# Load lag, batch-statistics chain and first-strip order in the output stage of a two-layer convolution and gating kernel

## What is computed

```
n  = groupnorm(x)
xc = n * channel_gate                      # one factor per image and channel
g  = sigmoid(y) + sigmoid(s)               # one factor per image and pixel (a scan y, a 7x7 convolution s)
x2 = xc * g
mean, var = x2.mean((0, 1, 2)), x2.var((0, 1, 2))       # over all images: one pair per channel
out = x + relu((x2 - mean) * rsqrt(var + 1e-5) * gamma + beta)
```

## Time and profile before

| what | value |
|---|---|
| median of 3 runs | 3327.27 us |
| lowest and highest | 3323.25 and 3329.84 us |
| span of the profiled execution, first to last instruction | 3373.7 us |
| busy share of the span: PE, DVE, ACT | 77%, 88%, 80% |
| moved by the DMA engines | 1227.97 MB, mean 364 GB/s |

### The profile page before, as it was taken

The page is one execution under the profiler, slowest core; times in us unless marked ns, Lnnn a source line. Parts: engine busy times, 40 slices in busy tenths (PEclk is TensorE's granted clock), DMA queues, the critical chain, the costliest instruction groups (busy, mean ns, idle before and its releaser), DMA issues. The chain is left out here.

```text
span 3373.7 us, 50742 instructions
## 1 busy us (share of the span) xinstructions
PE 2587.4 (77%) x17105; PEld 1657.5 (49%) x17105; DVE 2976.3 (88%) x4060; ACT 2701.0 (80%) x3772; POOL 56.8 (2%) x111
## 2 busy tenths in 40 slices
PE   7899999999999999999976333333776776766676
PEld 5566666666566666665432000000555555555555
DVE  8788999889998889988886999998999899888787
ACT  6788888888888888887763888887888888877777
POOL 3000000000000000000001100000000000000000
PEclk9999999999999999999986555555877778777767
DMA  8899999999999999998755999996999999999997
GB/s 318 328 374 399 386 367 366 364 368 401 374 364 365 369 398 384 366 367 335 274 129 122 380 420 419 420 421 261 382 428 430 428 426 420 415 386 374 373 369 289
DMA packets 199056, 1227.97 MB, mean 364 GB/s; under 512 B 29792, under 2 KB 38936, under 8 KB 157644
## 3 DMA queue, kind: packets, MB, share of 16 engines
q1 hardware_dynamic: 195884, 1223.41, 91.1%
q0 software_dynamic: 2976, 2.00, 0.3%
HBM read 805.14 MB, written 420.17 MB: 363 GB/s over the span
## 5 line engine op out<-in xcount | busy, mean ns | idle before, releaser
L1440 PE MATMUL psum<-signs,taps 128*128 128x448 f16 x4032 | 855.4, 355 | 29.4 <-DVE signs L1071 14.4
L1554 PE MATMUL psum<-signs,picked 12*128 12x448 bf16 x896 | 334.4, 517 | 340.4 <-DMA signs<-gate_scratch 276.6
L1945 ACT ACTIVATE stage<-psum 128x512 f32<-128x512 f32 x784 | 407.5, 614 | 209.1 <-DMA out_dram<-stage 186.7
L1440 PEld LDWEIGHTS psum<-signs,taps 128*128 128x128 f16 x4032 | 386.8, 98 | 351.7 <-issue 33.8
L1965 DVE SCALAR_TENSOR_TENSOR xc<-xt,curs,psum 128x1792 f32<-128x1792 f32 x222 | 452.0, 2077 | 121.7 <-PE psum L1554 119.2
L835 ACT ACTIVATE xt<-psum 128x896 f32<-128x896 f32 x416 | 378.0, 910 | 151.8 <-PE psum L1338 128.0
L1757 DVE SCALAR_TENSOR_TENSOR xc<-xt,curs,psum 128x1792 f32<-128x1792 f32 x224 | 455.8, 2077 | 34.0 <-PE psum L1554 33.1
L1691 ACT ACTIVATE xc<-xc 128x1792 f32<-128x1792 f32 x224 | 380.0, 1697 | 95.9 <-DVE xc L1757 95.9
L1122 DVE CUSTOM_DVE_ANT_0 xt<-scratch,xt 128x896 f32<-128x896 int8 x416 | 435.7, 1084 | 14.2 <-ACT scratch L843 14.2
L1338 PE MATMUL psum<-ident,stage 128*128 128x128 f32 x3066 | 410.2, 276 | 16.4 <-DMA stage<-x_dram 10.6
L1933 ACT ACTIVATE xc<-xc,bn,curs 128x1792 f32<-128x1792 f32 x224 | 411.1, 1899 | 7.6 <-DVE xc L1965 4.2
(11 more groups left out here) (222 smaller groups left out, 2830.4 us busy)
## 6 DMA issues: line engine op xcount, KB each, us to landing
xt<-x_scratch SPq DMA_DIRECT2D x210, 1792.0 KB
out_dram<-stage SPq DMA_DIRECT2D x112, 1792.0 KB, 13.6
stage<-x_dram SPq DMA_DIRECT2D x219, 896.0 KB, 9.0
xc<-x_scratch SPq DMA_DIRECT2D x210, 896.0 KB, 8.2
x_scratch<-xt SPq DMA_DIRECT2D x208, 896.0 KB, 8.5
x_scratch<-last_unit SPq DMA_DIRECT2D x16, 896.0 KB, 8.9
signs<-ssm_scratch SPq DMA_DIRECT2D x14, 448.0 KB, 4.6
xc<-ssm_scratch SPq DMA_DIRECT2D x14, 448.0 KB, 5.0
```

Of the source, the lines that this page charges most:

```text
L1440: return nc.tensor.matmul(turn[h % 2][:, b * 512:b * 512 + HB], taps[:, j, t, :], signs[:, j, r:r + RT // 2, dw:dw + W], start=t == 0, sto ...
L1554: last = nc.tensor.matmul(dst[:, b, :], picked[:, b * P:(b + 1) * P], gate_rows[:, s * BW:(s + 1) * BW], start=True, stop=True)
L1945: nc.scalar.activation(outs[n % 2][:, 2 * k:2 * k + 2, :].rearrange("p t c -> p (t c)"), out_ps[k % 4], ACT.Identity).then_inc(staged, 1)
```

## The change

It has three parts, all around the end of the third stage and in the output stage.

1. **SP's stream of the output stage** is written out for all 112 strips instead of a loop. At strip m it waits for `x2_made`, loads the gate row of strip m + 7, and then loads the next strips of x as far as `behind` lets it: strips 7 to 27 are loaded 7 strips ahead as before, strips 28 to 48 six ahead, and strips 49 to 111 five ahead. The store follows as before. The gate rows have semaphores of their own, `gates4`, for which PE's `spread` waits; DVE's `make_u` now waits for `arrived4`, which counts strips of x alone.
2. **The statistics chain.** Products of the scales with 1 / (number of pixels) are made early in the third stage (`gains`, in the tile `pair_counts`), which turns three products and a later scaling into one product. The refinement of the reciprocal root has two instructions of another kind in place of three. The scale is put on all of `par` by one instruction in place of two. Only the first half of u of the first strip is made ahead of the reductions; the second comes behind the chain, and so does the copy of the first image's row of `par` into `curs`, which stood at the head of the next block.
3. **The first two strips.** At strips 0 and 1 PE spreads the gate of strip m + 2 behind the fourth group of transposes of strip m, and DVE makes u of strip m + 1 after it has added strip m (before: at strip 0 only).

```diff
@@ third stage, DVE
+                nc.vector.tensor_scalar(gains[:, :, 0:NJ], par[:, :, NJ:2 * NJ], 1.0 / (NB * HW), None, ALU.mult
+                                        ).then_inc(gains_made, 1)
...
+                nc.vector.tensor_tensor(gains[:, :, NJ:2 * NJ], gains[:, :, 0:NJ], par[:, :, NJ:2 * NJ], ALU.mult
+                                        ).then_inc(gains_made, 1)
...
-                for j in range(NJ):
+
+                def first_strip(j):
                     nc.vector.scalar_tensor_tensor(
...
+                first_strip(0)
...
-                steps(nc.vector.tensor_tensor(wsum[:, :, 0:NJ], bnsum[:, :, 0:NJ], scales, ALU.mult))
-                steps(nc.vector.tensor_tensor(wsum[:, :, NJ:2 * NJ], bnsum[:, :, NJ:2 * NJ], scales, ALU.mult))
-                steps(nc.vector.tensor_tensor(wsum[:, :, NJ:2 * NJ], wsum[:, :, NJ:2 * NJ], scales, ALU.mult))
+                dve.wait_ge(gains_made, 2)
+                steps(nc.vector.tensor_tensor(wsum[:, :, :], bnsum[:, :, :], gains, ALU.mult))
...
-                steps(nc.vector.tensor_scalar(bn[:, 0:2, :], bn[:, 0:2, :], count, None, ALU.mult))
...
-                steps(nc.vector.tensor_tensor(t, t, rs, ALU.mult))
-                steps(nc.vector.tensor_scalar(t, t, -0.5, 1.5, ALU.mult, ALU.add))
-                steps(nc.vector.tensor_tensor(rs, rs, t, ALU.mult))
+                steps(nc.vector.scalar_tensor_tensor(t, t, -0.5, rs, ALU.mult, ALU.mult))
+                steps(nc.vector.scalar_tensor_tensor(rs, t, 1.5, rs, ALU.add, ALU.mult))
...
+                nc.vector.tensor_copy(curs[:, 0:1, :], par[:, NB - 1:NB, :]).then_inc(cur_made4, 1)
+                first_strip(1)
@@ output stage, SP
+                def behind(m):
+
+                    return min((m - NS) * 5 // (total - NS), 2)
...
+                fetched = NS
+                for m in range(total):
+                    sp.wait_ge(x2_made, 2 * (m + 1) + X4)
+                    if m + NS < total:
+                        load_gate(sp, gates4, ((m + NS) // NS - 1) % NB, m % NS)
+                    while fetched < total and fetched - NS + behind(fetched) <= m:
+                        fetch(fetched)
+                        fetched += 1
+                    sp.wait_ge(staged, (m + 1) * TG + E4)
@@ output stage, PE
-                        if n + 2 < NN or more:
+                        early = isinstance(it, int) and it == 0 and n < 2
+                        if not early and (n + 2 < NN or more):
                             spread(it, n + 2)
...
+                            if early and k == 3:
+                                spread(it, n + 2)
@@ output stage, DVE
+                    dve.wait_ge(arrived4[s], it * 32 + 16 * (n // NS + 1))
...
-                        first = isinstance(it, int) and it == 0 and n == 0
-                        if not first and (n + 1 < NN or more):
+                        early = isinstance(it, int) and it == 0 and n < 2
+                        if not early and (n + 1 < NN or more):
```

More of the change, by code:

```diff
@@ L1838, in binary_conv_then_gated_ssm_block @@
         arrived4 = [sem(f"arrived4_{s}") for s in range(NS)]
+        gates4 = [sem(f"gates4_{s}") for s in range(NS)]
         spread4 = sem("spread4")
-        cur_made4 = sem("cur_made4")
         u_made4 = sem("u_made4")
@@ L1889, in spread @@
                 def spread(it, n):
-                    pe.wait_ge(arrived4[n % NS], it * 64 + 32 * (n // NS + 1))
+                    pe.wait_ge(gates4[n % NS], it * 32 + 16 * (n // NS + 1))
                     pe.wait_ge(u_made4, it * (2 * NN) + 2 * n)
@@ L1969, in _ @@
                 dve.sem_inc(x2_made, X4)
-                nc.vector.tensor_copy(curs[:, 0:1, :], par[:, bass.ds(place(0, 0), 1), :]).then_inc(cur_made4, 1)
                 dve.wait_ge(cur_made4, 1)
@@ L1985, in step @@
                                                     slots[n % NS][:, :, j, :], ALU.add).then_inc(x2_made, 1)
-                        if first:
+                        if early:
                             make_u(it, n + 1)
```

35 lines of the change are left out of this document (15 added, 20 removed).

## The result

The changed kernel took **3352.42 us** (median of 5 runs, 3336.21 to 3358.22); the kernel before took 3325.80 beside it (5 runs, 3317.86 to 3329.84). The ratio is 1.0077 [1.0062, 1.0092]: slower, where 3318.0 was forecast. The executions of both kernels fall in two groups and a ratio leaves out those more than 1.5% above the fastest of their kernel, so I give beside each ratio how many lay over 3340 us, and the median of all.

A forecast was written before the change was run, and what follows sets the result against it. Transfers were taken to bound the kernel, with DVE close behind. Head 2.9 us (chain 0.75, first strips 2.1) plus lag 6.2 made 9.1 us off the 3327.3 median: 3318.2, stated as 3318.0, range 3311 to 3326.

The forecast's parts named there:

- The statistics chain: End of third stage: shorter chain and one half of u made later start relu 0.75 us earlier, ends 0.75 and 1.75.
- The first two strips: Output stage's start: first store at R+15.8, not R+18.2 (R: ACT's first relu); 2.1 us gained, 3.3 with faster PE.
- the faster variant: First strips, if PE's clock has risen: additions of strip 2 end 0.6 us earlier than before, instead of 0.6 later.
- The head: Statistics chain and first two strips together: 2.9 us gained, ends 2.9 and 5.0, all carried to the end.
- The lag: Output stage: strips 21 and 43 without loads save 9.9 us, late loads cost 3.6; net 6.2, ends 5.1 and 7.4.
- the rival that the lag gives nothing back: Output stage: compute cannot use the strips without a load, so only the head's gain remains, 3324.4 us; chance 0.20.
- SP's written-out stream: Output stage: gate row ahead of the load issues the load about 1 us later, which costs nothing with the queue full.
- slower, by the rate of the transfers: Output stage: changed addresses start the slow pace at strip 43 instead of 66, costing 27 us less 9: 3345; chance 0.09.

The follow-up runs named there:

- e9: Changed kernel with SP's output-stage loop of before and no lag, keeping the new statistics chain and first strips; 3323.87 us, ratio 0.9995.
- second trace of before: The kernel before, unchanged, profiled a second time, in an execution without the slow stretch; its time 3330.64 us.
- e6: Kernel before, its loop kept, with only the gate row issued ahead of the load in the output stage; 3327.66 us, ratio 1.0012.
- e7: Kernel before with SP's output-stage loop written out as straight code and nothing else; 3342.09 us, ratio 1.0052.
- e3: Changed kernel without the lag: SP's stream written out, every strip loaded 7 strips ahead; 3358.38 us, ratio 1.0054.
- e2: Changed kernel, run again beside the kernel before on the same chip; 3345.13 us, ratio 1.0027.
- e10: Changed kernel with SP's loop of before and the lag inside it (strips 6 and 13 without a load, then five ahead); 3314.79 us, ratio 0.9950.
- e15: Repeat of e10 on another chip; 3318.27 us, ratio 0.9979.
- e14: Kernel before with SP's output-stage loop as 3 turns of 28 strips in place of 6 of 14; 3384.88 us, ratio 1.0169.

## Why the prediction was wrong, point by point

**The statistics chain: size wrong, on the good side.** The changed kernel, same view as the earlier trace rows:

```profile
2328.97 0.19 ACT L1695 ACTIVATION_READ_ACCUMULATOR xc<-xc  x1
2329.19 1.08 DVE L1787 TENSOR_REDUCE bnsum<-scratch 128x16 f32<-128x112 f32 x4
2330.30 0.22 DVE L1794 TENSOR_TENSOR wsum<-bnsum,pair_counts 128x64 f32<-128x64 f32 x1
...
2333.16 0.19 DVE L1810 TENSOR_TENSOR par<-par,bn 128x32 f32<-128x32 f32 x1
2333.39 0.17 DVE L1812 COPY curs<-par 128x4 f32<-128x4 f32 x1
2333.47 2.07 DVE L1778 SCALAR_TENSOR_TENSOR xc<-xt,curs,psum 128x1792 f32<-128x1792 f32 x1
2336.11 3.65 ACT L1951 ACTIVATE xc<-xc,bn,curs 128x1792 f32<-128x1792 f32 x2 [4.16 <-DVEq L1991]
```

From the last sum of squares (2329.16) to relu 6.95 us, before 2350.95 - 2342.38 = 8.57: 1.62 us gained. The prediction chose 0.75 between ends of 0.75 and 1.75. Relu began 0.57 us behind the end of u (2335.54), not 1.0 and a copy behind it, so most of the barrier ran beside u. With what the Trainium skill says of sequencer instructions (PSUM — Partial Sum Buffer, Engine vs sequencer instructions) this row agrees: the gain is near the 1.75 that followed from it.

**The first two strips: right, with one order missed.** Counted from R, now 2336.11:

```profile
2342.05 3.68 PE L1926 MATMUL psum<-ident,last_unit 128*128 128x128 f32 x16 [4.24 <-DVE last_unit L2002]
2345.93 4.02 DVE L2002 TENSOR_TENSOR signs<-xc,xt 128x1792 f32<-128x1792 f32 x2
...
2351.91 0.37 SPq L1897 DMA_DIRECT2D out_dram<-stage  x1
2352.76 0.67 SPq L1885 DMA_DIRECT2D xt<-x_scratch  x1
2354.09 0.93 PE L1554 MATMUL psum<-signs,picked 12*128 12x448 bf16 x4
2355.06 4.07 DVE L1984 SCALAR_TENSOR_TENSOR xc<-xt,curs,psum 128x1792 f32<-128x1792 f32 x2 [1.13 <-PE psum L1554]
```

The first store is at R+15.8, as forecast (before R+18.2). The load of strip 8 is at R+16.65 and not R+14.3, since SP was still waiting for strip 0's staging when it could have been issued; the program's order shows that, and I had not followed it for SP. The DMA share is 0.48 from 2350 to 2355 us and 1.00 or more from there to 2370, so the engines are full soon behind the first store, as forecast. The additions of strip 2 end at R+26.9, with PE at the quicker clock (spread 0.93 us where the earlier trace rows has 1.65), 0.8 earlier than before; the faster variant said 0.6. The head alone is e9: its executions under 3340 are 3.0 us under those of the kernel before beside it (3323.3 against 3326.3). The forecast was 2.9, but the nearness is partly luck: the ratio's interval, 0.9985 to 1.0006, takes in no change, and the chain gave more than its term while the first strips gave less. From R to the end the traces without a slow stretch and without lag take 977.1, 978.1 and 977.4 us with the old first strips (second trace of before, e6, e7), 974.8 and 977.4 with the new ones (e3, e9), 1.5 us less on average where 2.1 was forecast.

**The lag: right in mechanism, and in size as far as the spread lets one see.** DVE behind the load that strip 21 leaves out (strips 24 and 25), and the chain of waits around it:

```profile
2542.54 3.95 DVE L2002 TENSOR_TENSOR last_unit<-xc,xt 128x1792 f32<-128x1792 f32 x2
2546.52 4.07 DVE L1984 SCALAR_TENSOR_TENSOR xc<-xt,curs,psum 128x1792 f32<-128x1792 f32 x2
2550.51 3.95 DVE L2002 TENSOR_TENSOR signs<-xc,xt 128x1792 f32<-128x1792 f32 x2
```

```profile
2520.86 12.87 DMA out_dram<-stage
2550.51 3.97 DVE signs L2002 x2
2558.58 3.88 DVE last_unit L2002 x2
2569.55 13.46 DMA out_dram<-stage
```

DVE runs at its floor (2542.54 to 2550.51, 7.97 us a strip), the chain goes through it for three strips, then back to the stores. The stores of strips 21 and 22 land after 9.2 and 8.6 us in place of 12.9 for strip 20, and that of strip 24 after 13.2, as forecast. e2 against e3 gives 5.3 us, e10 against e9 8.5, forecast 6.2. Head and lag together, in executions under 3340: 9.7 us in e2 (3326.5 beside it to 3316.8), 11.5 in e10 and 4.5 in e15, forecast 9.1. From R to the end the traces with lag and without the stretch take 972.3, 969.2 and 970.1 us (e2, e10, e15), against 974.8 and 977.4 without lag (e3, e9): 5.5 us on average, 2.5 to 8.2 by pairs. So the rival that the lag gives nothing back is out. Trace against trace, both with the slow stretch, R to the end fell from 1022.75 to 1014.59 us. What stands ahead of R varies between traces by more than all of this (R is 2336.1 to 2351.8 us, with 1.6 of it from the chain), so a few executions can't settle terms of this size.

**The step that failed** is the sentence on "SP's written-out stream": it weighed only where the gate row stands, and said of a load issued 1 us later that it "costs nothing". That the loop is gone was given no term. e7 has it alone: 6 of 12 executions over 3340, where the loop has 13 in 100. The 44 such executions of the written-out kernels that were not slowed lie at 3359.4 on average, 36 us over the other 26 (3323.0). Half of the executions more at 36 us each is 18 us on the mean, against 9.1 us gained. What in the written-out form brings them there stays open.

**The second failure is in the reading of the earlier trace rows and in the range.** The rows show that the same work can run at 426 and at 372 GB/s, and the span stood 46 us over the median, so the rate was known to differ between executions. The prediction tied it to the addresses (rival "slower, by the rate of the transfers"), gave it 0.09, and the range left it out. The price that this rival worked out, 3345, is near what came (3352.42 here, 3345.13 in e2) by luck; its mechanism is wrong: e3 has no lag and as many executions over 3340, and e10 has the lag and as few of them as the kernel before. Two things in hand would have warned: the profiled span lay far outside the three runs, so the slow stretch could strike a timed run as well; and three runs can't show how often it does.

## What to carry to other kernels

Where loads and stores share one queue and the engines are full, a faster kernel can still lose if its issue stream lets the engines fall in step, so time the form of the stream (loop or written out) by itself, with a dozen executions and a count of those that carry the loss. Keep a short loop where it exists and put a change inside it: e10 and e15 keep a gain, 0.9950 and 0.9979. Compare the packets of kind "instruction" in the two traces as well; here they rise with the share of slow executions. And before rows carry a prediction, set the profiled span beside the timed runs; where it lies outside, the difference may be a state that an edit makes rare or frequent.

## What the runs showed of the hardware that was not expected

- The 16 engines of one queue can work in step, all loading, then all storing: 370 GB/s in place of 421, a store of 1792 KB in 5.4 us beside a load in 4.4, and packets over 1000 ns 1 in 17 in place of 1 in 200. In the traces that have it, it begins at another strip in each and mostly stays to the last load; in e14 the rate came back from 374 to 409 GB/s.
- A left-out load does the same for a while: 392 GB/s and a share of 0.97 in 2700 to 2740, where the kernel before has 430 and 1.01. It passes: 429 from 2740 to 2780, and in e10, whose strips 6 and 13 have no load, 401 and 410 early and 428 from 2490 on.
- In the 28-strip loop two jumps back held SP for 6.42 and 6.05 us, with packets of kind "instruction" within; in the 14-strip loop a jump puts the load 1.0 to 1.1 us behind the store in place of 0.6.
- The Trainium skill (DMA: Bandwidth & Descriptors, Where 436 GB/s comes from) says that HBM binds transfers between it and the chip's memory at about 358 GB/s for a core, though it also quotes a measured 425. With one core at work, mixed loads and stores ran at 424 to 430 GB/s for hundreds of us here, and even in step at 370, so for one core the measurement decides; no run has a second core at work.
